# Keeping y in time order and reading it as a strided stationary operand in the attention output projection

## The chip, the cores and the metric

One core of one Trainium2 chip runs the kernel. The metric is the device time of one execution in microseconds (us). Every matmul here is in fp32 or in fp32r (a rounded fp32 that TensorE takes in one pass). To keep fp32 accuracy in fp32r, each operand is split into a high part (rounded to fp32r) and a low part (what is left), and each product is three matmuls: high by high, low by high, high by low.

## The reference, cut to what matters

Input x is 4 batches of 1024 tokens of 256 channels. Two layers follow each other:

```
x = x + retention(layernorm(x))        # 16 heads of 16 channels
x = x + ffn(layernorm(x))              # a shared gated MLP and 8 hash-routed experts
```

In `retention`, q, k and v are projections of x; scores q·k are decayed by gamma^(i-j) and masked to be causal; y is scores times v. y is then normalised over time and the channels of a head, scaled and shifted per channel, and multiplied by `W_o`:

```
yn = (y - mean) / sqrt(var + EPS) * gn_weight + gn_bias
out = yn @ W_o.T
```

The experts are routed by token index modulo 8, so in the second layer the tokens of a batch are taken in 8 groups ("slots") of 128 tokens: slot s holds the tokens whose index in time order is s modulo 8 (up to a fixed permutation of slots, done on the host).

## The kernel before, in words

**Stages.** Phase 1 goes through 16 parts (4 batches of 4 parts, 256 tokens each; `step(h)` with h from 0 to 15, b = h // 4 the batch and s = h % 4 the part in it). Phase 2 is the FFN, batch by batch (`shared` and `experts`). Each engine has its own instruction stream, written out by hand, and the streams are tied by semaphores; the order of the work on an engine is the order of the calls in its `step`.

**A part of phase 1 on TensorE** (`step`, lines 430 to 456): v, k and q of part h+1 are projected (36 fp32r matmuls of 256 columns, line 294, which is the helper `split_product` used for every split product), k is transposed (L343), x of part h+2 is transposed (L304); in parts with b > 0 work of the batch before is put in here (below); then `from_state` (L394) and `from_scores` (L403) give y of part h in PSUM (`y_bank`: 128 channels by 2 groups by 256 tokens, channels on partitions), and `scores(h+1)` (L364) and `state_sums(h+1)` (L379) prepare the next part.

**From y to the output projection.** y of a part leaves `y_bank` twice: ScalarE copies it to `yhi` (`high_y`, L617), VectorE computes y minus yhi into `ylo` (`low_y`, L812), and then takes the sums for the normalisation (`y_sums`, L817). `yhi` and `ylo` are laid out by slots: `[P, GROUPS, NE, P]`, that is for each of the 2 channel groups 8 slots of 128 tokens. So both instructions read PSUM with a step of 8 words (`slots_of_y`, L153) and write runs of 32 neighbouring words. The normalisation is folded into `W_o` (`wo_hi`, `wo_lo`), so y itself is never rewritten.

**The output projection** (`output`, L422 to 429) computes one output bank for 2 slots: for each of 2 slots 6 matmuls (2 channel groups by 3 split terms), 12 in all. y is the stationary operand (loaded as weights, 128 channels by 128 tokens of a slot), and `wo_hi` or `wo_lo` streams through as 256 columns. Each of the 12 matmuls loads its own weights: yhi, ylo, yhi. In phase 1, `output(b-1, j)` runs in the parts with s = 2 (j = 0, 1) and s = 3 (j = 2, 3): 24 matmuls in a row in parts 6, 7, 10, 11, 14 and 15. For the last batch all four calls, 48 matmuls, run between `shared(0, 3)` and `shared(0, 4)` of phase 2. VectorE adds the residual from the bank (`residual`, L861), which lets TensorE use the bank again (`scores` waits for `x1_ready`), and SyncE stores the sum (`store_x1`).

The buffers `yhi` and `ylo` are double: b % 2. ScalarE waits for `o_done` of two batches before when it writes them.

Of the kernel before, what the change touches and what calls it, by code (L numbers as in the profile page):

```python
# [5 lines left out]
F32 = mybir.dt.float32  # L6
F32R = mybir.dt.float32r
ALU = mybir.AluOpType
ACT = mybir.ActivationFunctionType

P = 128
NBATCH, T, D = 4, 1024, 256
CB = D // P
NH, DH = 16, 16
EPS = 1e-5
SUPER = 256
# [6 lines left out]
GROUPS = NH * DH // P  # L23
PAIRS = 4
NE = 8
# [28 lines left out]
def moe_retention(nc, xa, xs, wattn, gnw, gnb, sw1, sw3, sw2, w1, w2, sb1, sb3, b1, sb2, b2, decay, masks, out):  # L54
# [3 lines left out]
    with ExitStack() as ctx:  # L58
        def sem(name):
            return ctx.enter_context(nc.semaphore(name))  # L60
# [4 lines left out]
        p_bank, y_bank = banks[0:4], banks[4]  # L65
# [8 lines left out]
        def sb(name, shape, dt=F32, stack=ctx):  # L74
            return stack.enter_context(nc.sbuf_tensor(name, shape, dt))
# [29 lines left out]
        with ExitStack() as phase1:  # L105
            def sb_1(name, shape, dt=F32):
                return sb(name, shape, dt, phase1)

            xin = [sb_1(f"xin{i}", [P, TILES, D]) for i in range(NSUP)]
            dec = sb_1("dec", [P, 2, GROUPS, SUPER])  # L110
            wqkv_split = SplitWeight(nc, phase1, "wqkv", [P, 3, CB, D])
            xhi = sb_1("xhi", [P, CB, SUPER], F32R)
            xlo = sb_1("xlo", [P, CB, SUPER], F32R)
            kT = sb_1("kT", [P, GROUPS, SUPER])

            state = [sb_1(f"state{i}", [P, GROUPS, CPS + 1, 32]) for i in range(2)]
            qT = [sb_1(f"qT{i}", [P, GROUPS, SUPER]) for i in range(2)]
            keo = sb_1("keo", [P, CPS, GROUPS, 2, CH])
            kexp = sb_1("kexp", [P, CPS, GROUPS * PAIRS, 32])
            vexp = [sb_1(f"vexp{i}", [P, CPS, GROUPS * PAIRS, 32]) for i in range(2)]  # L120
            pm = [sb_1(f"pm{p}", [P, CPS * GROUPS, CH]) for p in range(PAIRS)]
            yhi, ylo = [None] * 2, [None] * 2
            for i in range(2):
                yhi[i] = sb_1(f"yhi{i}", [P, GROUPS, NE, P], F32R)
                if i:

                    with nc.sbuf_tensor("slot_scratch", [P, 2, D], F32) as slot_scratch:
                        pass
                ylo[i] = sb_1(f"ylo{i}", [P, GROUPS, NE, P], F32R)
            wo_raw = sb_1("wo_raw", [P, CB, D])  # L130
            wo_hi = sb_1("wo_hi", [P, CB, D], F32R)
            wo_lo = sb_1("wo_lo", [P, CB, D], F32R)
            y_bb = sb_1("y_bb", [P, GROUPS, P])
            o_bias = sb_1("o_bias", [P, D])
            sbias, bias7 = slot_scratch[:, 0, :], slot_scratch[:, 1, :]
# [13 lines left out]

        def const(name):  # L150
            return msk[:, slice(*MASK_COLS[name])]

        def slots_of_y():  # L153

            return y_bank[:].rearrange("p (g n s) -> p g s n", g=GROUPS, s=NE)

        def expert_buffer(e):
            return 3 if e == NE - 1 else e % 3
# [15 lines left out]
        sc_done, pm_ready, y_done, yhi_ready, ylo_ready, y_stats = (  # L174
            sem(n) for n in ("sc_done", "pm_ready", "y_done", "yhi_ready", "ylo_ready", "y_stats"))
# [112 lines left out]
        def _(pe):  # L288
            def split_product(o, w, x, first=True, last=True):

                n = len(w)
                for c in range(n):
                    for j, (l, r) in enumerate(((0, 0), (1, 0), (0, 1))):
                        mm = nc.tensor.matmul(o, w[c][l], x[c][r], start=first and c == 0 and j == 0,  # L294
                                              stop=last and c == n - 1 and j == 2)
                return mm
# [125 lines left out]
            def output(b, j, bank):  # L422
                if j == 0:
                    pe.wait_ge(ylo_ready, (b + 1) * NSUP)
                    pe.wait_ge(wolo_ready, b + 1)
                for i in range(2):
                    w = [(yhi[b % 2][:, c, 2 * j + i, :], ylo[b % 2][:, c, 2 * j + i, :]) for c in range(CB)]
                    mm = split_product(bank[:, i * D:(i + 1) * D], w, [(wo_hi[:, c, :], wo_lo[:, c, :]) for c in range(CB)])
                mm.then_inc(o_done, 1)

            def step(h):
# [20 lines left out]
                if b and s >= 2:  # L452
                    for j in range(2 * (s - 2), 2 * (s - 2) + 2):
                        pe.wait_ge(pm_ready, h * PAIRS + (j + 1))
                        output(b - 1, j, p_bank[j])
# [109 lines left out]
            for j in range(4):  # L565
                if j == 3:
                    pe.wait_ge(ob_copied, NBATCH)
                output(last, j, last_out_bank[j])
# [12 lines left out]
        def _(act):  # L581
# [29 lines left out]
            def high_y(h):  # L611
                b, s = h // NSUP, h % NSUP
                act.wait_ge(y_done, h + 1)
                if b > 1:
                    act.wait_ge(o_done, (b - 1) * 4)
                n = SUPER // NE
                nc.scalar.activation(yhi[b % 2][:, :, :, s * n:(s + 1) * n], slots_of_y(), ACT.Copy).then_inc(yhi_ready, 1)  # L617

            def high_wo(b):
                act.wait_ge(gn_a, b + 1)  # L620
# [20 lines left out]
            def step(h):  # L641
                b, s = h // NSUP, h % NSUP
                if b and s == 1:
                    high_wo(b - 1)
                if h + 1 < PARTS:
                    copy_v(h + 1)
                    spread_k(h + 1)
                    copy_k(h + 1)
                    if h + 2 < PARTS:
                        high_x(h + 2)  # L650
                else:
                    for j in range(4):
                        high_x2(0, j)
                if b and s == 1:
                    copy_bias(b - 1, p_bank[1])
                high_y(h)
                if h < 11:
                    high_ffn(h)
# [79 lines left out]
        def _(dve):  # L738
# [66 lines left out]

            def low_y(h):
                b, s = h // NSUP, h % NSUP
                at = slice(s * (SUPER // NE), (s + 1) * (SUPER // NE))
                if h == NSUP:
                    dve.wait_ge(bias_ready, 2)  # L810
                dve.wait_ge(yhi_ready, h + 1)
                nc.vector.tensor_tensor(ylo[b % 2][:, :, :, at], slots_of_y(), yhi[b % 2][:, :, :, at].bitcast(F32),  # L812
                                        ALU.subtract).then_inc(ylo_ready, 1)

            def y_sums(h):
                for g in range(GROUPS):
# [53 lines left out]
            def step(h):  # L870
# [32 lines left out]
                if h + 1 == PARTS:  # L903
                    low_x2(0, 2)
                    low_x2(0, 3)
                low_y(h)
                y_sums(h)
                if s == NSUP - 1:
# [279 lines left out]
```

## Time and profile before

| | us |
|---|---|
| median of 3 runs | 476.37 |
| lowest, highest | 472.18, 478.03 |
| the profiled execution, its own time | 476.37 |
| its span, first to last instruction | 474.6 |
| TensorE matmul busy | 444.9 (94%) |
| TensorE weight load busy | 413.7 (87%) |
| VectorE busy | 294.8 (62%) |
| ScalarE busy | 217.3 (46%) |
| GpSimd busy | 101.5 (21%) |

The profile is of one execution. In its lines, PE is TensorE's matmuls, PEld its weight loads (which can lie beside matmuls), DVE is VectorE, ACT ScalarE, POOL GpSimd, SP SyncE. L294 is line 294 of the kernel. `bank<-wo_hi,yhi` names the output, then the streamed operand, then the stationary one; "128*128" is rows by columns of the array that are used. Durations of matmuls and loads hold a fixed latency and overlap; the distance from one start to the next is what a stream of them costs.

### The profile page before, as it was taken

How to read it: one execution, taken by the hardware profiler on the slowest of the kernel's cores; microseconds unless marked ns; L12 is line 12 of the kernel's file. 1: busy time of each engine (PE TensorE's matmuls, PEld its weight loads, DVE VectorE, ACT ScalarE, POOL GpSimd, SP SyncE). 2: the span in 40 equal slices, each digit the busy share in tenths (PEclk: the TensorE clock that was granted, in tenths of full speed). 3: DMA queues.
4: the chain of work that ended last, by engine and by line, in shares of the span. 5: the costliest groups of instructions: out<-in, count | busy, mean ns of one | idle time of the engine just before them, and what ended most of it. 6: DMA issues, size and time to landing. Idle time of an engine off the chain costs nothing.

```text
span 474.6 us, 14932 instructions
## 1 busy us (share of the span) xinstructions
PE 444.9 (94%) x6574; PEld 413.7 (87%) x6574; DVE 294.8 (62%) x655; ACT 217.3 (46%) x416; POOL 101.5 (21%) x79
## 2 busy tenths in 40 slices
PE   6998869889989999986999999999999999999997
PEld 4988769789878999886788999889998899988996
DVE  6676886576687767788674654366544665456321
ACT  3564545435576463541333634346343553435521
POOL 2028221262134320141063110211102111030000
PEclk9998998889999899999999999999999999999999
DMA  7512151011442004020514001500005001030011
GB/s 263 187 52 70 69 157 68 17 57 69 157 157 70 4 3 180 10 86 3 186 81 178 1 0 47 221 1 0 33 11 221 0 0 44 0 133 0 1 46 44
DMA packets 9271, 34.75 MB, mean 73 GB/s; under 512 B 1665, under 2 KB 1921, under 8 KB 7041
## 3 DMA queue, kind: packets, MB, share of 16 engines
q1 hardware_dynamic: 8784, 33.15, 19.2%
q8 instruction: 45, 0.74, 0.6%
q10 hardware_dynamic: 432, 0.79, 0.5%
q14 instruction: 10, 0.07, 0.0%
HBM read 25.54 MB, written 8.39 MB: 71 GB/s over the span
## 4 chain that ended last, share of the span: by engine, by line
PE 88%; DVE 4%; issue 4%; DMA 1%; ACT 1%; POOL 0%; SPq 0%; DVEq 0%; ACTq 0%
PE bank L294 67%; PE bank L364 6%; PE bank L403 3%; PE bank L394 3%; PE bank L379 3%; PE bank L473 1%; PE bank L304 1%; DMA xin<-xa 1%; PE bank L343 1%; DVE pm L782 1%; PE bank L419 1%; DVE ln_st L917 1%; ACT kexp L592 0%; DVE kT L771 0%; DVE ylo L812 0%
## 5 line engine op out<-in xcount | busy, mean ns | idle before, releaser
L592 ACT ACTIVATE vexp<-bank 64x256 f32<-64x256 f32 x64 | 24.3, 379 | 67.6 <-PE bank L294 67.1
L688 ACT ACTIVATE xres<-bank,r1b 128x256 f32<-128x256 f32 x64 | 26.8, 469 | 55.5 <-PE bank L294 55.5
L294 PE MATMUL bank<-x2hi,sw_hi 128*128 128x512 f32 x128 | 51.0, 398 | 0.0
L294 PE MATMUL bank<-x2hi,sw_lo 128*128 128x512 f32 x128 | 50.9, 398 | 0.0
L673 ACT ACTIVATE sil<-bank,s1b 128x512 f32<-128x512 f32 x32 | 22.1, 689 | 63.0 <-PE bank L294 63.0
L294 PE MATMUL bank<-x2lo,sw_hi 128*128 128x512 f32 x128 | 50.3, 393 | 0.0
L949 DVE SCALAR_TENSOR_TENSOR gf<-bank,s3b,sil 128x512 f32<-128x512 f32 x32 | 24.0, 749 | 39.3 <-PE bank L294 39.3
L782 DVE TENSOR_TENSOR pm<-bank,msk 128x512 f32<-128x512 f32 x64 | 39.6, 681 | 2.7 <-PE bank L364 2.7
L364 PE MATMUL bank<-qT,keo 32*128 32x64 f32 x1024 | 34.5, 275 | 5.8 <-issue 3.9
L967 DVE TENSOR_TENSOR xr<-bank,xr 128x256 f32<-128x256 f32 x32 | 13.6, 424 | 41.8 <-PE bank L294 41.8
L364 PEld LDWEIGHTS bank<-qT,keo 32*128 32x128 f32 x1024 | 31.6, 187 | 8.1 <-issue 6.6
L294 PE MATMUL bank<-xhi,wqkv_hi 128*128 128x256 f32 x128 | 37.2, 291 | 1.3 <-DVE state L798 1.3
L294 PE MATMUL bank<-xhi,wqkv_lo 128*128 128x256 f32 x128 | 36.7, 287 | 0.0
L294 PE MATMUL bank<-xlo,wqkv_hi 128*128 128x256 f32 x128 | 36.5, 286 | 0.0
L294 PE MATMUL bank<-x2lo,w_hi 128*128 128x256 f32 x128 | 36.2, 283 | 0.0
L294 PE MATMUL bank<-x2hi,w_lo 128*128 128x256 f32 x128 | 36.2, 283 | 0.0
L294 PE MATMUL bank<-x2hi,w_hi 128*128 128x256 f32 x128 | 36.2, 283 | 0.0
L294 PE MATMUL bank<-sw_hi,ghi 128*128 128x256 f32 x128 | 36.1, 282 | 0.0
L961 DVE TENSOR_TENSOR elo<-xres,ehi 128x512 fp32r<-128x512 f32 x32 | 22.1, 691 | 22.5 <-ACT ehi L692 22.5
L294 PE MATMUL bank<-w_hi,elo 128*128 128x256 f32 x128 | 36.0, 282 | 0.0
L1093 POOL TENSOR_TENSOR xr<-xr,slot_bias 128x2048 f32<-128x2048 f32 x4 | 18.5, 4632 | 81.8 <-DMA xr<-x_scratch 81.8
L294 PE MATMUL bank<-w_lo,ehi 128*128 128x256 f32 x128 | 36.0, 281 | 0.0
(119 smaller groups left out, 1287.1 us busy)
## 6 DMA issues: line engine op xcount, KB each, us to landing
xin<-xa SPq DMA_DIRECT2D x16, 256.0 KB, 3.1
w_raw<-w SPq DMA_DIRECT2D x8, 512.0 KB, 4.2
xres<-xs SPq DMA_DIRECT2D x4, 1024.0 KB, 4.9
x_scratch<-xres SPq DMA_DIRECT2D x4, 1024.0 KB, 4.5
xl<-x_scratch SPq DMA_DIRECT2D x4, 1024.0 KB, 5.6
xr<-x_scratch SPq DMA_DIRECT2D x4, 1024.0 KB, 4.9
out<-xr SPq DMA_DIRECT2D x8, 512.0 KB, 2.6
sw_raw<-sw SPq DMA_DIRECT2D x3, 512.0 KB, 4.4
```

The lines of the kernel that those rows point to most:

```text
L294: mm = nc.tensor.matmul(o, w[c][l], x[c][r], start=first and c == 0 and j == 0, stop=last and c == n - 1 and j == 2)
L364: mm = nc.tensor.matmul(p_bank[p][:, o:o + CH], keo[at, c, g, :, :], qT[h % 2][at, g, c * CH:(c + 1) * CH], start=True, stop=True)
L379: mm = nc.tensor.matmul(b_bank[32 * p:32 * p + 32, o:o + n * 32].rearrange("p (n e) -> p n e", n=n), kexp[:, c, r, :], vexp[h % 2][:, c, r ...
L394: nc.tensor.matmul(y_bank[at, o:o + CH], state[h % 2][at, g, c, :], qT[h % 2][at, g, c * CH:(c + 1) * CH], start=(c == first and g == 0), ...
L403: mm = nc.tensor.matmul(y_bank[32 * p:32 * p + 32, o:o + CH], vexp[h % 2][:, c, g * PAIRS + p, :], pm[p][:, c * GROUPS + g, :], start=Fals ...
L592: cp = nc.scalar.activation(dst[64 * h2:64 * h2 + 64, :, f, :, h2, :], src[64 * f:64 * f + 64, :, :, h2, :], ACT.Copy)
L673: nc.scalar.activation(sil[i % 2][:], h1_bank[i % 2][:], ACT.Silu, bias=s1b[:, m:m + 1]).then_inc(sil_ready, 1)
L688: ge = nc.scalar.activation(hf[q % 2][:, m, :], e_bank[q % 4][:, m * 2 * P:(m + 1) * 2 * P], ACT.Gelu, bias=r1b[:, e, m:m + 1])
L782: nc.vector.tensor_tensor(pm[p][:], p_bank[p][:].rearrange("p (a i) -> p a i", i=CH), causal.unsqueeze(1).broadcast_to([P, CPS * GROUPS, C ...
L949: nc.vector.scalar_tensor_tensor(gf[i % 3][:], h3_bank[i % 2][:], s3b[:, m:m + 1], sil[i % 2][:], ALU.add, ALU.mult).then_inc(gf_ready, 1)
L961: nc.vector.tensor_tensor(elo[k][:], hf[q % 2][:], ehi[k][:].bitcast(F32), ALU.subtract).then_inc(elo_ready, 1)
L1093: nc.gpsimd.tensor_tensor(xr[:], xr[:], slot_bias[:], ALU.add).then_inc(biased, 1)
```

## The change: layout of yhi and ylo, and who reads with a step

`yhi` and `ylo` become `[P, GROUPS, T]` in time order. The two instructions that fill them read PSUM in order and write 256 neighbouring words per group. The output projection takes the 128 tokens of a slot out of the time-ordered buffer: its stationary operand is now read with a step of 8 words (32 bytes). The number of instructions, their order, the waits and the memory used stay as they are.

```diff
-                yhi[i] = sb_1(f"yhi{i}", [P, GROUPS, NE, P], F32R)
+                yhi[i] = sb_1(f"yhi{i}", [P, GROUPS, T], F32R)
...
-                ylo[i] = sb_1(f"ylo{i}", [P, GROUPS, NE, P], F32R)
+                ylo[i] = sb_1(f"ylo{i}", [P, GROUPS, T], F32R)
...
-        def slots_of_y():
-
-            return y_bank[:].rearrange("p (g n s) -> p g s n", g=GROUPS, s=NE)
...
-                    w = [(yhi[b % 2][:, c, 2 * j + i, :], ylo[b % 2][:, c, 2 * j + i, :]) for c in range(CB)]
+                    hi, lo = (y[b % 2][:].rearrange("p g (n s) -> p g s n", s=NE) for y in (yhi, ylo))
+                    w = [(hi[:, c, 2 * j + i], lo[:, c, 2 * j + i]) for c in range(CB)]
...
-                n = SUPER // NE
-                nc.scalar.activation(yhi[b % 2][:, :, :, s * n:(s + 1) * n], slots_of_y(), ACT.Copy).then_inc(yhi_ready, 1)
+                nc.scalar.activation(yhi[b % 2][:, :, s * SUPER:(s + 1) * SUPER], y_bank[:].rearrange("p (g i) -> p g i", g=GROUPS),
+                                     ACT.Copy).then_inc(yhi_ready, 1)
...
-                at = slice(s * (SUPER // NE), (s + 1) * (SUPER // NE))
+                at = slice(s * SUPER, (s + 1) * SUPER)
...
-                nc.vector.tensor_tensor(ylo[b % 2][:, :, :, at], slots_of_y(), yhi[b % 2][:, :, :, at].bitcast(F32),
-                                        ALU.subtract).then_inc(ylo_ready, 1)
+                nc.vector.tensor_tensor(ylo[b % 2][:, :, at], y_bank[:].rearrange("p (g i) -> p g i", g=GROUPS),
+                                        yhi[b % 2][:, :, at].bitcast(F32), ALU.subtract).then_inc(ylo_ready, 1)
```

## Rows read from the trace of the kernel before

**Rows 1.** The page: busy time by engine, and the chain that ended last.
```profile
PE 444.9 (94%) x6574; PEld 413.7 (87%) x6574; DVE 294.8 (62%) x655; ACT 217.3 (46%) x416; POOL 101.5 (21%) x79
...
PE 88%; DVE 4%; issue 4%; DMA 1%; ACT 1%; POOL 0%; SPq 0%; DVEq 0%; ACTq 0%
```

**Rows 2.** The chain in order of time, part 6 (start us, us, what).
```profile
93.12 0.86 PE bank L419 x4
...
101.89 5.11 PE bank L294 x36
...
107.87 2.87 PE bank L294 x24
110.73 1.03 PE bank L394 x64
...
112.79 1.94 PE bank L364 x64
...
115.76 4.50 PE bank L294 x36
```

**Rows 3.** PSUM readers by group and form: busy us, mean ns, idle before.
```profile
L766 DVE TENSOR_TENSOR xlo<-bank,xhi 128x512 fp32r<-128x512 f32 x16 | 11.1, 691 | 13.4 <-ACT xhi L584 13.4
L812 DVE TENSOR_TENSOR ylo<-bank,yhi 128x512 fp32r<-128x512 f32 x16 | 11.0, 687 | 8.7 <-ACT yhi L617 8.6
L937 DVE TENSOR_TENSOR x2lo<-bank,x2hi 128x512 fp32r<-128x512 f32 x16 | 10.6, 684 | 2.7 <-ACT x2hi L665 2.4 <-ACT x2hi L663 0.3
L584 ACT ACTIVATE xhi<-bank 128x512 fp32r<-128x512 f32 x16 | 9.6, 597 | 1.9 <-PE bank L304 1.5
L617 ACT ACTIVATE yhi<-bank 128x512 fp32r<-128x512 f32 x16 | 9.6, 597 | 20.5 <-PE bank L403 20.2
```

**Rows 4.** Tiles yhi, ylo: loads of y; duration ns min/median/max, first and last start.
```profile
L294 PEld LDWEIGHTS bank<-wo_hi,yhi x64: 188/190/192, 107.6 to 250.1; 128*128 128x128 f32 x64
...
L294 PEld LDWEIGHTS bank<-wo_lo,yhi x64: 187/192/192, 107.8 to 250.3; 128*128 128x128 f32 x64
...
L294 PEld LDWEIGHTS bank<-wo_hi,ylo x64: 187/192/192, 107.7 to 250.2; 128*128 128x128 f32 x64
```

**Rows 5.** Lines L364, L394 and L403: weight loads, same columns as rows 4.
```profile
L364 PEld LDWEIGHTS bank<-qT,keo x1024: 181/187/328, 16.6 to 221.0; 32*128 32x128 f32 x171
...
L394 PEld LDWEIGHTS bank<-qT,state x960: 101/105/105, 24.9 to 229.6; 32*32 32x32 f32 x192
...
L403 PEld LDWEIGHTS bank<-pm,vexp x1024: 106/110/110, 25.7 to 230.6; 128*32 128x32 f32 x171
```

**Rows 6.** Timeline of TensorE, 512-column matmuls (start us, us, engine, line).
```profile
239.03 0.40 PE L294 MATMUL bank<-x2hi,sw_hi 128*128 128x512 f32 x1
...
240.43 0.40 PE L294 MATMUL bank<-x2hi,sw_hi 128*128 128x512 f32 x1
```

**Rows 7.** Timeline of all engines in part 14, after its output projection.
```profile
215.28 1.09 PE L394 MATMUL bank<-qT,state 32*32 32x64 f32 x64
...
217.87 1.29 DVE L861 TENSOR_TENSOR xres<-bank,xres 128x512 f32<-128x512 f32 x2
...
219.31 2.01 PE L364 MATMUL bank<-qT,keo 32*128 32x64 f32 x64 [1.90 <-DVE xres L861]
```

**Rows 8.** The slowest reader by element: GpSimd's largest group, by form.
```profile
L1067 POOL TENSOR_TENSOR w_lo<-w_raw,w_hi 128x1024 fp32r<-128x1024 f32 x8 | 19.0, 2373 | 20.3 <-ACT w_hi L639 20.3
```

**Rows 9.** Stretches: busy by engine, granted clock, DMA share, GB/s.
```profile
98.00:99.00 1.00, 0.00 (x0) 0.00 (x0) 1.00 (x2) 0.00 (x0) 1.00 (x2) 1.00 0.00 0
...
101.00:102.00 1.00, 1.00 (x53) 0.94 (x44) 1.00 (x3) 0.00 (x0) 1.00 (x1) 0.50 0.02 8
...
107.60:110.60 3.00, 3.00 (x27) 2.93 (x25) 1.92 (x8) 2.17 (x6) 0.71 (x1) 1.00 0.47 178
```

## The prediction, made before the changed kernel was run

> **What bounds the kernel now.** I read the page first. TensorE is busy for 94% of the span and holds 88% of the chain that ended last; no other engine has over 4% of it [rows 1]. So whatever lengthens a stream of matmuls lengthens the kernel unless the time comes out of a wait, and whatever shortens ScalarE or VectorE gives nothing unless TensorE waits there. Next I read the chain in order of time around one output projection. In part 6 the 24 matmuls of line 294 from 107.87 on are followed at 110.73 by `from_state`, with nothing between; scores and the projections of the next part come as closely [rows 2]. The output projection is on the path with its full length.
>
> Last I asked which instructions touch y. Three groups of 64 weight loads take it as stationary operand, 192 loads, each for a matmul of 256 columns [rows 4]. The code has as many: 4 batches by 4 calls by 12 matmuls is 192.
>
> **The change part by part.**
>
> *ScalarE's and VectorE's copies.* They lose the step of 8 words in PSUM and write in longer runs. The row shows what the step costs today: the copy to yhi takes 597 ns, the copy to xhi, same size and without a step, 597 ns. The subtraction into ylo takes 687 ns, those into xlo and x2lo, without a step, 691 and 684 [rows 3]. The largest difference to any of these is 4 ns, 16 x 4 ns = 0.06 us over the kernel. I cost this part at nothing.
>
> *The weight loads of y.* The trace has no load of weights with a step, so I need the price of a plain one, what it hides behind, and bounds. A load of 128 columns takes 187 ns and one of 32 columns 105 ns, both of 32 rows; with 128 rows the 128 columns take 190 and the 32 columns 110 [rows 4, 5]. So each column costs (187 - 105) / 96 = 0.85 ns, or (190 - 110) / 96 = 0.83 ns, and a load streams for some 128 x 0.84 = 108 ns; the rest is latency, which overlaps. The matmuls of 256 columns start every 2.87 / 24 = 0.120 us [rows 2]. Those of 512 columns start every (240.43 - 239.03) / 6 = 0.233 us [rows 6], which makes 0.442 ns for a streamed column and 0.113 us for 256 of them. Load (108 ns) and stream (113 ns) run side by side and are nearly equally long. There is hardly cover: 5 to 12 ns.
>
> That a load can be what sets the distance is seen in the scores. They stream 64 columns like `from_state` and four run beside each other in separate rows; the group of four takes 4 x 1.94 / 64 = 0.121 us with 128 columns to load, and 4 x 1.03 / 64 = 0.064 us with 32 [rows 2]. So the distance is about the load's 108 ns plus 13 ns where the load is the longer one.
>
> Bounds of a load with a step of 8 words. Below: no more than today, 0 us; the copy to yhi reads PSUM with this very step at (597 ns over 512 elements) 1.17 ns each and loses nothing [rows 3]. Less than nothing is excluded, since the load without a step is already in order. Above: the slowest reader of SBUF in the trace, GpSimd's subtraction of 1024 elements in 2373 ns, 2.3 ns an element [rows 8]: 128 x 2.3 = 294 ns, 307 with the 13, 187 more than today's 120, and 192 x 187 = 35.9 us.
>
> The sum: load 2 x 108 = 216 ns, distance 229 ns, 109 ns more than 120; 192 x 109 ns = 20.9 us. By 227 ns it is 120 ns and 23.0 us.
>
> The Trainium skill speaks of such a step. In "SBUF — State Buffer" (Door 1: The DMA port swizzle, the note on cachelines) SBUF has lines of 16 bytes, and each access that goes to a new line pays. In "Vector Engine (DVE) Microarchitecture Reference" (The SBUF access granule: adjacent pairs) an access without a neighbour took 1.73 ns where neighbours take 1.05. Transferred to the load, 1.73 ns would be an estimate of 221 ns and 192 x 114 ns = 22 us. No row here has such an access to SBUF.
>
> *What is given back.* In each of parts 6, 7, 10, 11, 14 and 15 TensorE gets 24 x 109 ns = 2.6 us more, for the last batch 5.2 us. After the projections of part 14 it waits today: y is done with L403 by 217.4, but scores start at 219.31, released by the residual on VectorE, which had work of its own until 217.87 [rows 7]. TensorE will come there at 217.4 + 2.6 = 220.0; the residual of the second bank needs matmuls that now end near 217.9, just when VectorE is free for it. So the 1.9 us of waiting go, and part 14 pays 0.7. In the other parts TensorE goes on without a wait, as in part 6 [rows 2], and pays in full. The store of x1 moves with the residual and has no reader before the experts. Sum: 20.9 - 1.9 = 19.0 us.
>
> The execution profiled took 476.4 us (span 474.6 and 1.8 around it), which is also the median: 476.4 + 19.0 = 495.4, rounded 495.
>
> **The rivals.**
>
> *The step is free for loads (not slower).* A load takes a column per 0.84 ns, about the pace at which ScalarE reads PSUM with this step for nothing [rows 3, 5], and if a fetch brings two words or fewer, TensorE's limit of 0.442 ns a word leaves room for one fetch per column (0.88 ns, 113 ns in all, where the matmul takes 113 as well). What speaks against it is that it is PSUM, not SBUF. Then 192 distances stay at 120 ns, or grow to 113 + 13 = 126: 0 to 1.2 us, and 476.4 to 477.6. It decides for itself if the load stays under the stream plus its overhead. "TensorE: Matmul & The Clock Gate" of the Trainium skill (LDWEIGHTS) has a load depend on its number of columns alone, which would give this result; the columns' part agrees with rows 5, a step is in no row.
>
> *The load pays more than double.* If every column needs a fetch of its own, VectorE, ScalarE and the streamed operand compete for the same memory, and a column comes to 2.3 ns as at GpSimd [rows 8]: 35.9 - 1.9 = 34 us, 510. For it speaks only that the step is short, against it that GpSimd reads two operands. The same DVE page of the Trainium skill has 2.50 ns for one short step (24 words), which would be 320 ns and 39 us by estimate.
>
> *The clock falls as well.* When TensorE stood still at 98, its granted clock fell from 1.00 to 0.50, that is from 2.4 to 1.2 GHz, some microseconds later, and the 36 matmuls at 101.89 took 5.11 us where those at 115.76 took 4.50 [rows 2, 9]. During the projection the clock is 1.00 now [rows 9]. If an array that is half idle in the seven stretches counts as idle, each costs 0.6 us, and if the whole following stretch of 36 ran at half, up to 36 x 0.1 = 3.6; I take 1.4: 495 + 10 = 505. Against it: the matmuls don't stop.
>
> **Chances.** Doubling, 491 to 500: 0.42. Free step: 0.33, of which 0.03 is for a measurement over 2% lower. More than double: 0.15. Clock as well: 0.10. A measurement tells 2% from no change, that is 9.5 us, 485.9. Faster 0.03, same 0.30, slower 0.67. The range takes in the free step and most of the upper bound: 473 to 511; the likeliest case's own range is 491 to 500. The predicted time is that of the doubling, 495.
>
> **What would show it.** Right: loads of y last longer by some 110 ns (190 to 300) while the loads of other operands stay at 188 to 192; the stretch of 24 matmuls in part 6 goes from 2.87 to about 5.5 us and the 48 of the last batch from 5.8 to 11; the copy to yhi stays at 597 ns and the subtraction at 687; the wait for the residual in part 14 is gone. Wrong: loads of y at 190 and stretches of 2.87 us (free step); matmuls at 0.3 us distance (more than double); a granted clock under 1.00 in or behind the projections (clock). If the loads are longer but the stretches aren't, my statement that there is no cover falls.

## The result, and the profile after

The changed kernel takes 500.47 us (median of 4 runs, 495.65 to 501.4) where the one before, measured beside it, takes 475.69 (472.18 to 478.03): ratio 1.051, 95% interval 1.041 to 1.060. It is 24.8 us slower; 495 had been forecast, within 473 to 511. Medians here and below are of all runs; ratios and intervals leave out the executions in which the chip ran in a slower state. The profiled execution took 499.69 us with a span of 497.8, 23.2 more than the span of 474.6 before.

The page of the changed kernel, busy time by engine and the chain. It answers to [rows 1]; line 294 is now L290, since the diff removes four lines above it.

```profile
PE 466.5 (94%) x6574; PEld 435.6 (87%) x6574; DVE 296.9 (60%) x655; ACT 217.1 (44%) x416; POOL 101.4 (20%) x79
...
PE 89%; issue 4%; DVE 4%; ACT 1%; DMA 1%; POOL 0%; DVEq 0%; ACTq 0%
```

The same 6574 matmuls keep TensorE busy for 21.6 us more; ScalarE, VectorE and GpSimd do what they did. The shares say nothing of this: TensorE is at 94% before and after.

The chain of the changed kernel in order of time, around part 6, part 15 and the last batch. It answers to [rows 2].

```profile
108.40 5.80 PE bank L290 x24
114.20 1.02 PE bank L390 x64
...
116.25 1.94 PE bank L360 x64
...
239.77 5.80 PE bank L290 x24
...
259.73 53.94 PE bank L290 x348
```

And the last of these before, the same 348 matmuls, 48 of which are the output projection:

```profile
242.15 48.26 PE bank L294 x348
```

A stretch of 24 went from 2.87 to 5.80 us, six times 2.93 = 17.6 us, and the stretch of 348 grew by 5.7. (The chain before passes by the projections of part 14; their matmuls started 0.12 us apart there too.) Together 23.3 us; the span grew by 23.2. In part 6 the scores behind the projection still take 1.94 us, so there nothing but the projection itself has become longer.

The tiles yhi and ylo of the changed kernel (duration ns min/median/max), against [rows 3, 4]:

```profile
L290 PEld LDWEIGHTS bank<-wo_hi,yhi x64: 312/337/341, 108.1 to 273.0; 128*128 128x128 f32 x64
...
L290 PEld LDWEIGHTS bank<-wo_lo,yhi x64: 335/338/341, 108.6 to 273.4; 128*128 128x128 f32 x64
...
L613 ACT ACTIVATE yhi<-bank x16: 597/597/598, 26.7 to 248.6; 128x512 fp32r<-128x512 f32 x16
L809 DVE TENSOR_TENSOR ylo<-bank,yhi x16: 677/690/692, 27.4 to 249.2; 128x512 fp32r<-128x512 f32 x16
```

A load of y lasts 338 ns instead of 190. The two copies, which lost their step in PSUM, take what they took: 597 ns, and a mean of 687 ns for the subtraction (the 690 above is its median; before, the same view had 692).

### The profile page after: what moved, and what is told of

It reads as the page before. It is cut to its first block, busy times and chain, and to the rows that moved or that the text cites. A ratio compares the mean times of both kernels' runs of the same rounds, so it can differ in the third digit from the quotient of the medians.

```text
span 497.8 us, 14932 instructions
## 1 busy us (share of the span) xinstructions
PE 466.5 (94%) x6574; PEld 435.6 (87%) x6574; DVE 296.9 (60%) x655; ACT 217.1 (44%) x416; POOL 101.4 (20%) x79
## 4 chain that ended last, share of the span: by engine, by line
PE 89%; issue 4%; DVE 4%; ACT 1%; DMA 1%; POOL 0%; DVEq 0%; ACTq 0%
PE bank L290 69%; PE bank L360 6%; PE bank L399 3%; PE bank L390 3%; PE bank L375 3%; PE bank L300 1%; PE bank L470 1%; PE bank L339 1%; DVE pm L779 1%; DMA xin<-xa 1%; PE bank L415 1%; DVE xin L758 1%; ACT kexp L589 0%; DVE ln_st L745 0%; DVE kT L768 0%
## 5 line engine op out<-in xcount | busy, mean ns | idle before, releaser
L290 PE MATMUL bank<-x2hi,sw_lo 128*128 128x512 f32 x128 | 51.0, 398 | 0.0
L290 PE MATMUL bank<-x2hi,sw_hi 128*128 128x512 f32 x128 | 50.9, 398 | 0.0
L290 PE MATMUL bank<-x2lo,sw_hi 128*128 128x512 f32 x128 | 50.2, 392 | 0.0
L360 PE MATMUL bank<-qT,keo 32*128 32x64 f32 x1024 | 35.5, 278 | 4.7 <-issue 4.7
L290 PE MATMUL bank<-xhi,wqkv_hi 128*128 128x256 f32 x128 | 37.3, 291 | 1.5 <-DVE state L795 1.5
L290 PE MATMUL bank<-xhi,wqkv_lo 128*128 128x256 f32 x128 | 36.6, 286 | 0.0
L290 PE MATMUL bank<-xlo,wqkv_hi 128*128 128x256 f32 x128 | 36.4, 284 | 0.0
L290 PE MATMUL bank<-x2lo,w_hi 128*128 128x256 f32 x128 | 36.2, 283 | 0.0
L290 PE MATMUL bank<-x2hi,w_hi 128*128 128x256 f32 x128 | 36.2, 283 | 0.0
L290 PE MATMUL bank<-x2hi,w_lo 128*128 128x256 f32 x128 | 36.2, 283 | 0.0
L290 PE MATMUL bank<-sw_hi,ghi 128*128 128x256 f32 x128 | 36.1, 282 | 0.0
L290 PE MATMUL bank<-w_hi,elo 128*128 128x256 f32 x128 | 36.1, 282 | 0.0
L290 PE MATMUL bank<-w_lo,ehi 128*128 128x256 f32 x128 | 36.0, 281 | 0.0
L290 PE MATMUL bank<-w_hi,ehi 128*128 128x256 f32 x128 | 35.9, 281 | 0.0
L290 PE MATMUL bank<-sw_lo,ghi 128*128 128x256 f32 x128 | 35.8, 280 | 0.0
```

The costliest lines, as they stand in the source:

```text
L360: mm = nc.tensor.matmul(p_bank[p][:, o:o + CH], keo[at, c, g, :, :], qT[h % 2][at, g, c * CH:(c + 1) * CH], start=True, stop=True)
```

## The experiments

Twelve runs were made, of eleven kernels; one ran twice. My theory: every column of a load with a step of 8 words is a fetch of its own of about 1.8 ns, a fetch brings four neighbouring words, and nothing covers the excess. The rivals: the copies or the layout have a part in it; any column without a neighbour pays, or the price follows the step; load and stream use one path.

**Which part of the change costs, and from which step.** The first three kernels keep the changed kernel's layout and copies and change only which words a load takes (k is the step; each kernel has its number written out):

```diff
-                    hi, lo = (y[b % 2][:].rearrange("p g (n s) -> p g s n", s=NE) for y in (yhi, ylo))
-                    w = [(hi[:, c, 2 * j + i], lo[:, c, 2 * j + i]) for c in range(CB)]
+                    at = slice((2 * j + i) % (8 // k) * k * P, ((2 * j + i) % (8 // k) + 1) * k * P, k)
+                    w = [(yhi[b % 2][:, c, at], ylo[b % 2][:, c, at]) for c in range(CB)]
```

Step 1:

> The changed kernel with its copies (y in time order), but the loads of y take 128 neighbouring words, so they take other tokens than the reference wants. If the loads with a step are the whole cost, the time is that of the kernel before (475.7 us, ratio 1.00) and the stretches of 24 matmuls take 2.87 us. If the copies or the layout cost anything, some of the 24 us stay.

Step 2:

> As the run with neighbouring words, but the loads of y have a step of 2 words (other tokens than the reference wants). Theory of four-word fetches: 64 fetches for 128 columns, about 115 ns, still under the stream; ratio 1.00, matmuls 0.12 us apart. Rival, a word pays as soon as it has no neighbour in the access: full price at step 2 already, matmuls 0.24 us apart, some 499 us. Rival, price in proportion to the step: 0.12 us at 2, 0.18 at 4.

Step 4:

> As before with a step of 4 words (other tokens than the reference wants). Four-word fetches: one fetch for each column, full price, matmuls 0.24 us apart, ratio 1.05 as with step 8. Price in proportion to the step: some 0.18 us and 487 us.

Beside a kernel before at 476.90 us they took, as medians, 477.48, 477.62 and 499.83 us; the ratios are 0.999 (0.994 to 1.004), 1.004 (1.000 to 1.007) and 1.049 (1.043 to 1.054). Their loads of yhi, step 1, then 2, then 4:

```profile
L290 PEld LDWEIGHTS bank<-wo_hi,yhi x64: 188/190/337, 108.3 to 253.9; 128*128 128x128 f32 x64
```
```profile
L290 PEld LDWEIGHTS bank<-wo_hi,yhi x64: 193/195/198, 106.3 to 249.6; 128*128 128x128 f32 x64
```
```profile
L290 PEld LDWEIGHTS bank<-wo_hi,yhi x64: 308/329/337, 110.1 to 275.1; 128*128 128x128 f32 x64
```

With step 1 the loss is gone, to within 0.6%, while layout and copies stay, so it is the loads. A step of 2 leaves them at 195 ns, and a step of 4 costs nearly what a step of 8 does (329 ns against 338). A price that goes on growing with the step and a price for any column without a neighbour both fall.

**All steps in one kernel.** The steps differ by call of `output`, twelve matmuls each:

```diff
+STEPS = ((1, 2, 3, 4), (5, 6, 7, 8), (9, 10, 12, 14), (15, 16, 1, 8))
...
+                    k = STEPS[b][j]
+                    w = []
+                    for c in range(CB):
+                        first = c * (T if k <= NE else NE)
+                        w.append(tuple(y[b % 2][:].rearrange("p g t -> p (g t)")[:, first:first + (P - 1) * k + 1:k] for y in (yhi, ylo)))
```

> The steps of the loads of y differ by call, twelve matmuls each (other tokens than the reference wants): 1, 2, 3, 4 in the first batch, 5 to 8 in the second, 9, 10, 12, 14 in the third, 15, 16, 1, 8 in the last. Four-word fetches: twelve matmuls take 1.4 us at 1 and 2, about 2.2 us at 3 (96 fetches), 2.9 us from 4 on, whatever the step. If banks of memory clash, even or large steps (8, 16) cost more than odd ones (9, 15). If the price is for any access without a neighbour: 2.9 us from 2 on.

The timeline of TensorE in part 7 of it: step 3 from 121.93, step 4 from 124.11 (start us, us, engine, line).

```profile
122.19 0.34 PE L291 MATMUL bank<-wo_hi,ylo 128*128 128x256 f32 x1
...
123.94 0.34 PE L291 MATMUL bank<-wo_lo,yhi 128*128 128x256 f32 x1
124.11 0.39 PE L291 MATMUL bank<-wo_hi,yhi 128*128 128x256 f32 x1
124.34 0.40 PE L291 MATMUL bank<-wo_hi,ylo 128*128 128x256 f32 x1
...
126.47 0.40 PE L291 MATMUL bank<-wo_hi,ylo 128*128 128x256 f32 x1
```

From 122.19 to 123.94 lie ten starts, 0.175 us each; from 124.34 to 126.47 nine, 0.237 each. Read like this, the distance in ns is

| step | 1 | 2 | 3 | 4 | 5 | 6 | 7 | 8 | 9 | 10 | 12 | 14 | 15 | 16 |
|---|---|---|---|---|---|---|---|---|---|---|---|---|---|---|
| ns | 120 | 120 | 175 | 237 | 227 | 228 | 235 | 242 | 240 | 234 | 262 | 243 | 229 | 222 |

The 262 at step 12 is not to be compared with the rest. It was taken in part 15, where the granted clock was 0.50 at first (stretch, with the clock as the third figure from the end, and first and last start in it at that clock):

```profile
235.90:238.20 2.30, 2.30 (x11) 2.30 (x9) 2.06 (x6) 0.77 (x2) 0.00 (x0) 0.50 0.03 7
```
```profile
236.28 0.47 PE L291 MATMUL bank<-wo_hi,ylo 128*128 128x256 f32 x1
...
237.89 0.47 PE L291 MATMUL bank<-wo_hi,ylo 128*128 128x256 f32 x1
```

Six distances of 268 ns at 0.50; the few of step 12 that follow at 1.00 lie between 240 and 270.

Step 3 is the telling one: 128 columns three words apart touch 96 groups of four words, three quarters of the 128 groups at step 4, and its distance is 175 where step 4 has 237. From 4 on every column has a group of its own and the price is level within a tenth (222 to 243, step 12 left out). The step of 16 is the cheapest of them, that of 9 is no cheaper than that of 8: no clash of large or even steps, step 12 again left open.

**Fewer columns.** In the changed kernel the loads take 128, 96, 64 and 32 columns:

```diff
+                    m = (128, 96, 64, 32)[j]
+                    w = [(h[:, 0:m], l[:, 0:m]) for h, l in w]
-                    mm = split_product(bank[:, i * D:(i + 1) * D], w, [(wo_hi[:, c, :], wo_lo[:, c, :]) for c in range(CB)])
+                    mm = split_product(bank[0:m, i * D:(i + 1) * D], w, [(wo_hi[:, c, :], wo_lo[:, c, :]) for c in range(CB)])
```

> The changed kernel with its step of 8, but the loads of y take 128, 96, 64 and 32 columns in the calls j = 0 to 3 (the rest of the output's rows isn't computed). If each column is a fetch of some 1.8 ns, matmuls are 0.24, 0.18, 0.12 and 0.12 us apart: at 64 columns and fewer the stream covers the load. If a load with a step pays a fixed price, 0.24 us throughout.

Timeline of TensorE, the first and last matmuls of 128, 96, 64 and 32 columns:

```profile
110.52 0.40 PE L290 MATMUL bank<-wo_hi,ylo 128*128 128x256 f32 x1
...
112.94 0.40 PE L290 MATMUL bank<-wo_lo,yhi 128*128 128x256 f32 x1
...
113.36 0.35 PE L290 MATMUL bank<-wo_hi,ylo 128*96 128x256 f32 x1
...
115.19 0.35 PE L290 MATMUL bank<-wo_lo,yhi 128*96 128x256 f32 x1
...
126.13 0.29 PE L290 MATMUL bank<-wo_hi,ylo 128*64 128x256 f32 x1
...
127.36 0.29 PE L290 MATMUL bank<-wo_lo,yhi 128*64 128x256 f32 x1
127.48 0.28 PE L290 MATMUL bank<-wo_hi,yhi 128*32 128x256 f32 x1
...
128.77 0.28 PE L290 MATMUL bank<-wo_lo,yhi 128*32 128x256 f32 x1
```

Ten distances each (eleven for the last): 242, 183, 123 and 117 ns. From 128 to 96 columns it falls by 59 ns, 1.84 ns a column (1.81 over all four batches, 241 against 183), and at 64 the load of 64 x 1.81 = 116 ns is about as long as the stream. So at a step of 8 the distance is 1.81 ns a column and 9 ns, and not less than the stream's 117 to 120. The fit is close, not exact: it gives 125 ns for 64 columns (measured 123) and, put on the 96 groups of step 3, 183 (measured 175). With the same 9 ns, the steps from 3 to 16 come to 1.66 to 1.83 ns a group.

**One load in three.** Only ylo is in time order; yhi stays by slots. A further line of the edit, not shown, lets VectorE write ylo in time order while it reads by slots, so its write now has the step of 8 words:

```diff
-                ylo[i] = sb_1(f"ylo{i}", [P, GROUPS, NE, P], F32R)
+                ylo[i] = sb_1(f"ylo{i}", [P, GROUPS, T], F32R)
...
-                    w = [(yhi[b % 2][:, c, 2 * j + i, :], ylo[b % 2][:, c, 2 * j + i, :]) for c in range(CB)]
+                    lo = ylo[b % 2][:].rearrange("p g (n s) -> p g s n", s=NE)
+                    w = [(yhi[b % 2][:, c, 2 * j + i, :], lo[:, c, 2 * j + i]) for c in range(CB)]
```

> Only ylo is in time order and loaded with a step of 8; yhi stays by slots. 64 of the 192 loads have the step. If nothing covers the excess, each costs 122 ns: 7.8 us, 483.5 us, ratio 1.016. If a plain load ahead of it gives a load with a step a start (the two buffers for weights), less: under 4 us.

Timeline of TensorE, first comparison:

```profile
109.24 0.28 PE L294 MATMUL bank<-wo_hi,yhi 128*128 128x256 f32 x1
109.36 0.40 PE L294 MATMUL bank<-wo_hi,ylo 128*128 128x256 f32 x1
109.60 0.28 PE L294 MATMUL bank<-wo_lo,yhi 128*128 128x256 f32 x1
109.72 0.28 PE L294 MATMUL bank<-wo_hi,yhi 128*128 128x256 f32 x1
```

The matmul with ylo takes 0.24 us, its two neighbours 0.12: a plain load ahead gives no start at this clock. In part 15, at a granted clock of 0.50, it looks otherwise (from one matmul with ylo to another, both at that clock):

```profile
230.69 0.42 PE L294 MATMUL bank<-wo_hi,ylo 128*128 128x256 f32 x1
...
232.63 0.42 PE L294 MATMUL bank<-wo_hi,ylo 128*128 128x256 f32 x1
```

Nine distances of 0.216 us, and none of them stands out: with one load in three, the step costs next to nothing over the 0.213 us that plain loads take at 0.50 (the section on the prediction has them).

The run changes a second thing, VectorE's write:

```profile
L813 DVE TENSOR_TENSOR ylo<-bank,yhi x16: 1077/1090/1160, 27.6 to 237.4; 128x512 fp32r<-128x512 f32 x16
```

It lasts 1090 ns where it took 692 before. In part 15 it is on the chain, 1.16 us where it was 0.69. So this run is clean evidence for the distance of the matmuls, not for the time of the kernel.

The whole kernel came out at a ratio of only 1.009 (1.003 to 1.014), which is 4 us and not 7.7. So it ran once more:

> The kernel in which ylo alone is loaded with a step, once more, since its stretches in the trace say 64 times 0.12 us = 7.7 us and the first comparison said 4 us with an interval to 6.7. If the excess is on the path as in the changed kernel, less the wait of 1.9 us in part 14 that goes first: 6 us, ratio 1.013. If something else gives time back, 1.008 again.

This time 484.74 us against 476.32, ratio 1.017 (1.011 to 1.022). The two intervals overlap between 1.011 and 1.014, about 6 us. The kernel itself had nearly the same median both times (485.22 and 484.74); what moved was the kernel before, 479.15 and 476.32. Of the wait in part 14 it keeps 0.93 of 1.90 us, so 1.0 us is given back and the timeline says 6.7 us, and some tenths more for VectorE's write. The comparison alone can't tell 6 from 8 us.

**Do load and stream lie side by side?** Each matmul streams 512 columns instead of 256, once in the kernel before and once in the changed one:

```diff
+                    x = [tuple(t[:].rearrange("p c d -> p (c d)") for t in (wo_hi, wo_lo))] * CB
-                    mm = split_product(bank[:, i * D:(i + 1) * D], w, [(wo_hi[:, c, :], wo_lo[:, c, :]) for c in range(CB)])
+                    mm = split_product(bank[:], w, x)
```

> The kernel before, but each matmul of the output projection streams 512 columns (both halves of W_o) into a whole bank, so it computes other sums than the reference. Matmuls 0.233 us apart, as the others of 512 columns; 192 times 113 ns is 22 us more than before, some 497 us.

> The same with the changed kernel's loads with a step of 8 (other sums than the reference). If load and stream lie side by side, the longer one counts: matmuls 0.24 to 0.25 us apart, at most 3 us more than the run with plain loads. If the load's fetches take turns with the stream's on one path, the excess of 122 ns comes on top: 0.35 us apart, 22 us more.

One run each: 502.0 us with plain loads, 502.4 with the step. Timeline of TensorE, plain loads, then step 8:

```profile
111.88 0.39 PE L294 MATMUL bank<-wo_hi,ylo 128*128 128x512 f32 x1
...
114.19 0.39 PE L294 MATMUL bank<-wo_lo,yhi 128*128 128x512 f32 x1
```
```profile
107.94 0.41 PE L290 MATMUL bank<-wo_hi,ylo 128*128 128x512 f32 x1
...
110.38 0.41 PE L290 MATMUL bank<-wo_lo,yhi 128*128 128x512 f32 x1
```

Ten distances: 231 ns and 244 ns, which is 2.5 us for 192 loads. The whole stretches say more. In the chain, part 6, plain loads and then step 8:

```profile
111.81 5.49 PE bank L294 x24
```
```profile
107.73 6.00 PE bank L290 x24
```

Over all seven stretches the difference is 3.8 us, more than the 3 us I had allowed. The whole runs, one each and 0.4 us apart, can't tell. So the same 192 slow loads that cost 23 us cost about 4 when 512 columns stream beside them. What is lost is cover, not a resource that both use up.

**The streamed operand with a step.** The kernel before, `W_o` read with steps of 1, 2, 4, 8, then in a second kernel in runs:

```diff
+                    k = (1, 2, 4, 8)[j]
+                    x = [tuple(t[:, c].rearrange("p (a s) -> p s a", s=k) for t in (wo_hi, wo_lo)) for c in range(CB)]
+                    mm = split_product(bank[:, i * D:(i + 1) * D].rearrange("p (s a) -> p s a", s=k), w, x)
```

> The kernel before with plain loads; the streamed W_o is read with a step of 1, 2, 4 and 8 words in the calls j = 0 to 3 (its columns are permuted in the output, which the reference does not want). If each fetch takes about 1.8 ns and brings four neighbouring words, 256 columns take 0.12 us at step 1, 0.24 at 2 (128 fetches), 0.46 to 0.48 at 4 and 8. If only loads pay, 0.12 us throughout.

> The kernel before with plain loads; the streamed W_o is read in runs of 2 words with a hop of 8 (j = 0), runs of 4 with a hop of 16 (j = 1), single words with a step of 16 (j = 2) and of 32 (j = 3), its columns permuted in the output, which the reference does not want. If the stream fetches pairs of words at 0.88 ns: 0.12, 0.12, 0.23, 0.23 us. If it fetches lines of four at 1.77 ns, which would not fit the 0.23 us at step 4 and 8 seen before unless two are open at once: 0.12 us only at j = 1, 0.23 at j = 0.

First and last starts at step 2 and step 8 in the first kernel, part 6 and part 7:

```profile
111.53 0.41 PE L294 MATMUL bank<-wo_hi,ylo 128*128 128x256 f32 x1
...
113.80 0.41 PE L294 MATMUL bank<-wo_lo,yhi 128*128 128x256 f32 x1
...
127.28 0.41 PE L294 MATMUL bank<-wo_hi,ylo 128*128 128x256 f32 x1
...
129.46 0.41 PE L294 MATMUL bank<-wo_lo,yhi 128*128 128x256 f32 x1
```

Ten distances: 227 ns at step 2 and 218 at step 8; read the same way, 119 at step 1 and 233 at step 4. The second kernel: runs of 2 words with a hop of 8 take 234 ns, runs of 4 with a hop of 16 take 115, single words with steps of 16 and 32 take 220 and 222. My expectation of 0.46 us at steps 4 and 8 failed, and so did a fetch of pairs, since pairs cost 234. The stream pays double as soon as it doesn't use groups of four whole, and no more in any pattern tried.

**Both with a step of 8:**

```diff
+                    x = [tuple(t[:, c].rearrange("p (a s) -> p s a", s=8) for t in (wo_hi, wo_lo)) for c in range(CB)]
+                    mm = split_product(bank[:, i * D:(i + 1) * D].rearrange("p (s a) -> p s a", s=8), w, x)
```

> Loads of y and streamed W_o both with a step of 8 (the output's columns are permuted, which the reference does not want). If the two are read on separate paths, matmuls stay 0.24 us apart as with the loads alone. If both use up one path, the sum counts: some 0.34 us (0.12 plus 0.12 for the load's and 0.10 for the stream's excess) or more.

Timeline of TensorE:

```profile
110.35 0.42 PE L290 MATMUL bank<-wo_hi,ylo 128*128 128x256 f32 x1
...
112.77 0.42 PE L290 MATMUL bank<-wo_lo,yhi 128*128 128x256 f32 x1
```

Ten distances of 242 ns, as with the loads alone. The one run took 504.6 us. Load and stream don't add up: the longer one counts.

## Why the prediction was right

*TensorE is the bound and nothing gives at the copies.* Held: ScalarE at 597 ns and VectorE at 687 as before, and step 1 in the changed layout is level with the kernel before.

*192 loads, hardly any cover.* Held: 64 loads with a step give a third of the effect in the timeline, and the excess all but vanishes beside 512 columns or with 64 columns to load.

*A doubling, 229 ns a matmul, 20.9 us.* The mechanism was right and the size too small. The term "2 x 108 = 216 ns" measured 128 x 1.81 = 232, and the overhead "13 ns" measured 9: 241 ns, 192 x 121 = 23.3 us. The duration of a load, forecast to grow by some 110 ns, grew by 148. The variant in the text with one fetch of 1.77 ns for a column, 23.0 us, was the better one; I took the rounder number. The way to 1.77, though, is not shown by the runs. It compared line 419 with an fp32r stream by equal array work, two passes of fp32 in 0.215 us. The trace has 16 records of line 419 for its 8 calls, each with its own weight load and 256 columns; that one record of 0.215 us holds two passes is in no row. And it was taken from the stream, at 0.442 ns a word for four words, and a stream with one word of four takes 222 / 256 = 0.87 ns for it, not 1.77. For loads the group of four and its price of 1.7 to 1.8 ns are measured; that it is the stream's limit too was a guess.

The Trainium skill's "SBUF — State Buffer" (Door 1: The DMA port swizzle, the note on cachelines) wants two uses of each line of 16 bytes for full pace. For loads the runs agree: 120 ns at step 2, 175 at step 3, 222 to 243 from step 4 on (step 12 left out). Its next clause, that one can step up to 4 fp32 for free, does not hold for them. For the stream two words of a line are too few: 227 ns against 119. "TensorE: Matmul & The Clock Gate" (LDWEIGHTS), by which a load depends on its columns alone, is wrong for a step over 2: 338 ns against 190 for the same 128 columns.

*Given back in part 14, 1.9 us.* Half right. The timeline of the changed kernel there, against [rows 7]:

```profile
230.46 1.09 PE L390 MATMUL bank<-qT,state 32*32 32x64 f32 x64
...
232.51 1.11 PE L360 MATMUL bank<-qT,keo 32*128 32x64 f32 x30
...
234.69 1.32 PE L360 MATMUL bank<-qT,keo 32*128 32x64 f32 x34 [1.06 <-issue]
```

From `from_state` to the first scores it took 4.03 us before and takes 2.05 now: the wait for the residual is gone, 2.0 us. But the scores stop in the middle for 1.06 us, with nothing in the profile that they wait for; before, they ran through. The other runs say when it comes. The line of the run with one load in three:

```profile
223.27 2.01 PE L364 MATMUL bank<-qT,keo 32*128 32x64 f32 x64 [0.93 <-DVE xres L862]
```

With 0.62 to 1.90 us of the wait left at the granted clock of 1.00, the scores of part 14 run through in 2.01 us (the kernel before, step 2, one load in three twice, and the first kernel with a strided stream). With 0.58 us left they take 2.45 (the second kernel with a strided stream), and in each of the seven runs without the wait 0.5 to 1.1 us longer than 2.01, 1.06 here and mostly 0.6. So the stop comes when the wait goes, and the wait is not given back whole; what the stop itself waits for stays open. Part 14 gave back 2.0 less 1.06, that is 0.9 us. The projections at 23.3 less 0.9 would be 22.4; the span grew by 23.2, and the 0.8 us between were not followed; single stretches differ by as much from one execution to the next (36 matmuls at 101.60 took 5.93 us, at 101.89 before 5.11). So 19.0 was 20.9 less 1.9, and the measured 24.8 (with an interval of 20 to 29) holds 23.3 less 0.9; the rest is not told from noise.

*The time and the range.* The likeliest case had 491 to 500 for its own range, and 500.47 lies just outside. It had a chance of 0.42, the free step 0.33, and 473 to 511 would have taken in both. That 500.47 lies in that range says little; the loads at 338 ns, the stretches at 5.80 and the copies as before are what bears the mechanism out.

*The rivals.* A free step fell with the first load's duration. More than double fell too: 1.81 ns a column, 2.15 times the plain 0.84, and not 2.3 ns. The clock was not what cost the time: the profiled execution had a mean granted clock of 0.979, the one before 0.978, and it was 1.00 in the projections except in part 15. There TensorE had stood still until 239.11; the kernel with step 1 had 0.50 in part 15 too, the kernel before had 1.00, so the fall does not need a load with a step. That stretch shows something of its own (stretches: TensorE busy, weight loads, VectorE, ScalarE, GpSimd, then the granted clock):

```profile
242.00:243.00 1.00, 1.00 (x6) 1.00 (x5) 0.14 (x1) 0.00 (x0) 0.00 (x0) 0.50 0.00 0
```

and the timeline of TensorE in it, changed kernel:

```profile
242.07 0.44 PE L290 MATMUL bank<-wo_hi,ylo 128*128 128x256 f32 x1
...
243.04 0.45 PE L290 MATMUL bank<-wo_lo,yhi 128*128 128x256 f32 x1
```

At 0.50, that is at 1.2 GHz, the matmuls with loads of step 8 start 0.24 us apart as at 2.4 GHz. In the kernel with step 1, part 15 also ran at 0.50, and there they start 0.213 us apart instead of 0.12:

```profile
227.00:229.50 2.50, 2.50 (x13) 2.50 (x12) 2.08 (x6) 0.77 (x2) 0.00 (x0) 0.50 0.03 7
```
```profile
227.79 0.41 PE L290 MATMUL bank<-wo_hi,yhi 128*128 128x256 f32 x1
...
229.07 0.41 PE L290 MATMUL bank<-wo_hi,yhi 128*128 128x256 f32 x1
```

So at a step of 8, the price of a load with a step does not follow TensorE's clock. At step 12 it may in part: 268 ns at 0.50.

## What to carry to other kernels

Lay a stationary operand out so that a load reads neighbouring words, or at most every second one; do the permutation where the data is copied out of PSUM, where a step of 8 words in what is read cost nothing on ScalarE or VectorE. In what VectorE writes to SBUF the same step took 1090 ns instead of 692. Before a load is made slower, compare it with the stream beside it: by the estimates above 128 columns need 108 ns plain and 213 to 234 with a step of 4 words or more, 256 streamed columns cover about 115 ns, 512 cover 230. Price an operand's layout per load and multiply by the loads: the buffer was written 16 times and loaded 192 times.

## What the runs showed of the hardware that was not expected

A load of fp32r pays by groups of four words, 1.81 ns a group at step 8 and 1.7 to 1.8 at the others, and 96 groups for 128 columns at step 3 show it; a stream pays double (0.85 to 0.91 ns a word instead of 0.45) for anything but whole groups of four, pairs included, and no more at the steps tried up to 32. Both can pay at the same time without adding up (242 ns). And at a step of 8 a matmul stays at 0.24 us when the granted clock is halved, so at 1.2 GHz the step costs 27 ns and at 2.4 GHz 121; with only one load in three it costs next to nothing at 1.2 GHz (0.216 us against 0.213). Why load and stream differ, at step 2 and from 4 on, stays open.
